# A prefetch hint on the closing branch of the four engines' loops over images

## The reference, cut to what matters

```python
x = _L0_conv_ref(x, ...)        # group norm, q/k/v, softmax(q k^T / sqrt(128)) v over 1024 points, projection, x + out
t = _to_tokens(x)               # 1024 tokens of 128 numbers
t = t + _L1_attn_ref(_ln_t(t), ...)   # 8 search heads x 2 retrievers of width 16, softmax over 1024 keys, gate, w_out
t = t + _L1_ffn_ref(_ln_t(t), ...)    # two 128x128 maps, one dequantised from 4 bits
x = _from_tokens(t, x)
```

## Time and profile before

| | |
|---|---|
| median of 3 executions | 5834.74 us (5830.56 to 5835.21) |
| the profiled execution | 5838.83 us, span 5836.5 us |
| busy: TensorE | 5436.7 us (93%), 30350 matmuls |
| busy: GpSimd | 4251.2 us (73%), 1109 instructions |
| busy: VectorE | 3955.0 us (68%), 8189 instructions |
| busy: ScalarE | 3470.2 us (59%), 6689 instructions |
| mean granted TensorE clock | 0.981 |

### The profile page before, as it was taken

The page is one execution under the profiler, slowest core; times in us unless marked ns, Lnnn a source line. Parts: engine busy times, 40 slices in busy tenths (PEclk is TensorE's granted clock), DMA queues, the critical chain, the costliest instruction groups (busy, mean ns, idle before and its releaser), DMA issues.

```text
span 5836.5 us, 99943 instructions
## 1 busy us (share of the span) xinstructions
PE 5436.7 (93%) x30350; PEld 3295.9 (56%) x30350; DVE 3955.0 (68%) x8189; ACT 3470.2 (59%) x6689; POOL 4251.2 (73%) x1109
## 2 busy tenths in 40 slices
PE   5999999999999999999999999999999999999986
PEld 3555555565555555555555555555555555556543
DVE  4776667667676666676667676677766676766763
ACT  2566566656566565666565665666665656665654
POOL 1677777777777777777777777777777777777787
PEclk9999999999999999999999999999999999999998
DMA  1101110111111111111111111111111111101110
GB/s 36 24 26 33 31 38 26 27 34 27 38 26 34 27 34 30 37 26 30 31 27 38 31 29 27 34 30 38 26 34 27 27 37 36 28 24 36 23 33 11
DMA packets 64867, 176.65 MB, mean 30 GB/s; under 512 B 21856, under 2 KB 23264, under 8 KB 64224
## 3 DMA queue, kind: packets, MB, share of 16 engines
q1 hardware_dynamic: 64224, 168.61, 12.3%
HBM read 17.53 MB, written 16.78 MB: 6 GB/s over the span
## 4 chain that ended last, share of the span: by engine, by line
PE 79%; DVE 9%; ACT 5%; issue 4%; POOL 2%; SPq 0%; DMA 0%; DVEq 0%; ACTq 0%; POOLq 0%
PE ps_bank L776 16%; PE ps_u L810 16%; PE ps_bank L799 15%; PE ps_bank L763 7%; PE ps_bank L691 4%; PE ps_bank L679 3%; DVE max_part L1062 3%; DVE max_part L1072 3%; PE ps_bank L747 2%; PE ps_bank L819 2%; PE ps_bank L750 2%; PE ps_bank L749 2%; PE ps_bank L748 2%; POOL p_sum L627 2%; ACT work L963 2%
## 5 line engine op out<-in xcount | busy, mean ns | idle before, releaser
L627 POOL TENSOR_TENSOR p_sum<-p_sum,p 128x2048 f32<-128x2048 f32 x768 | 3509.0, 4569 | 411.4 <-ACT p L982 381.2
L1072 DVE TENSOR_REDUCE max_part<-ps_bank 128x1 f32<-128x512 f32 x4096 | 2613.7, 683 | 1237.9 <-PE ps_bank L776 1224.9
L982 ACT ACTIVATE p<-ps_bank 128x512 f32<-128x512 f32 x4096 | 2283.6, 599 | 1495.3 <-PE ps_bank L799 1482.6
L799 PE MATMUL ps_bank<-q_stack,k_stack 128*128 128x512 f32 x4096 | 1726.3, 438 | 25.1 <-DVE t_front L1096 20.7
L776 PE MATMUL ps_bank<-k_stack,q_stack 96*128 96x512 f32 x4096 | 1594.6, 426 | 25.9 <-DVE max_part L1072 11.2
L776 PEld LDWEIGHTS ps_bank<-k_stack,q_stack 96*128 96x128 f32 x4096 | 777.6, 193 | 687.5 <-DVE max_part L1072 287.2
L627 POOL TENSOR_TENSOR p_sum<-p 128x2048 f32<-128x2048 f32 x128 | 584.3, 4565 | 792.4 <-ACT den_sb L990 731.3
L799 PEld LDWEIGHTS ps_bank<-q_stack,k_stack 128*128 128x128 f32 x4096 | 766.2, 192 | 655.1 <-issue 273.2
L810 PE MATMUL ps_u<-p,rv 128*32 128x512 f32 x8192 | 1114.5, 617 | 19.1 <-ACT u_sb L987 12.2
L763 PEld LDWEIGHTS ps_bank<-v,p 128*128 128x128 f32 x4096 | 494.1, 191 | 17.8 <-issue 2.4
L763 PE MATMUL ps_bank<-v,p 128*128 128x129 f32 x4096 | 498.2, 274 | 1.6 <-ACT p L939 1.6
(11 more groups left out here) (140 smaller groups left out, 4600.2 us busy)
## 6 DMA issues: line engine op xcount, KB each, us to landing
q_stack<-q_hi SPq DMA_DIRECT2D x256, 128.0 KB, 2.4
k_stack<-k_hi SPq DMA_DIRECT2D x512, 64.0 KB, 2.3
x_sb<-in_x SPq DMA_DIRECT2D x32, 512.0 KB, 3.3
t_held<-t_front SPq DMA_DIRECT2D x32, 512.0 KB, 2.9
k_stack<-k_lo SPq DMA_DIRECT2D x256, 64.0 KB, 2.4
q_stack<-q_lo SPq DMA_DIRECT2D x128, 128.0 KB, 2.3
t_core<-t_held SPq DMA_DIRECT2D x32, 512.0 KB, 3.4
out_y<-out_sb SPq DMA_DIRECT2D x32, 512.0 KB, 2.6
```

Source lines behind the costliest of these rows:

```text
L627: pool.tensor_tensor(p_sum[:, :, :], before, p1[:, step % ring, :, :], ALU.add)\
L799: pe.matmul(out, k_stack[:, head, keys], q_stack[:, head // 2, queries], start=True, stop=True)\
L982: act.activation(p1[:, step % ring, n, :], read_bank(), ACT.Exp, scale=scale1)\
L1072: dve.tensor_reduce(max_part1[:, i, n, half:half + 1], read_bank(), AXIS.X, ALU.max)\
```

## The change

`in_order` gets `nc` as its first argument, opens the loop through it with the same bounds and the one engine, and asks for a hint.

```diff
-def in_order(engine, steps, images, stages, banks=None, links=None, first=None):
+def in_order(nc, engine, steps, images, stages, banks=None, links=None, first=None):
...
     before = links.count if links else 0
-    with engine.Fori(1, images - 2) as b:
+    with nc.Fori(1, images - 2, engines=[engine.engine], hint_back_edge=True) as b:
         if banks:
             banks.looped = (b - 1) * (banks_per_image // BANKS)
...
-                in_order(pool, steps, images, {"values": add_weights, "norm_group_var": rstd0,
+                in_order(nc, pool, steps, images, {"values": add_weights, "norm_group_var": rstd0,
                                                "ln1_stats": rstd_shift(0), "ln2_stats": rstd_shift(1)})
...
-                in_order(pe, steps, images, stages, banks, first=first_of_image)
+                in_order(nc, pe, steps, images, stages, banks, first=first_of_image)
...
-                in_order(act, steps, images, stages, banks)
+                in_order(nc, act, steps, images, stages, banks)
...
-                in_order(dve, steps, images, stages, banks, links)
+                in_order(nc, dve, steps, images, stages, banks, links)
```

## The result

The changed kernel takes 5740.45 us in the median of 4 runs (5738.39 to 5743.39); the kernel before took 5833.13 us beside it. The ratio is 0.9842, with a 95% interval of 0.9825 to 0.9859: 93 us or 1.6% faster. The forecast was 5728 us, in a range of 5690 to 5765. The profiled execution took 5743.39 us, 95.4 us less than the one of before, where the sum said 107.

What follows compares the result with a forecast made beforehand. TensorE was taken to bound the kernel, idling at each loop branch and then running at a lower clock. 5838.8 - 85 (idle) - 22 (clock) = 5732 us for the profiled execution, 5728 us as a median; range 5690 to 5765.

Steps and rivals of the forecast that it cites:

- The bound and the gap: TensorE's 28 "issue" waits before L747, 87.7 us, come from its loop branch; the hint saves 85 us.
- The step behind it: Round's end on TensorE: branch, way to L747 and hint take 0.53 us, hidden behind 0.65 us of queued work.
- What is late next: Round's start: L810, L799 and L819 have 0.7, 0.6 and 4.9 us to spare, so no wait replaces the gap.
- ScalarE and VectorE: At the back edge: their hints cost nothing; unhinted, ScalarE would be 1.5 us late at L939, mostly soaked up by six banks.
- The clock: TensorE's lower clock goes behind the back edge but comes near L715 in 20 of 28 rounds: 22 us saved.
- The last round and the tail: Last branch falls through though hinted as taken: nothing in the sum, 4 us kept for the range.
- The hint without effect: Rival at the loop branch: hint forgotten or its fetch thrown out; 5837 us, chance 0.09.
- Code displaced ahead of the branch: Rival "slower": target's fetch displaces code of L747 to L784, costing 88 us; 5922 us, chance 0.04.
- The shrunken stall: Rival at the round's start: target or next block late, half of the 3.13 us stays; 5781 us, chance 0.07.

Runs made afterwards that it cites:

- e12: As e9, but the hint on TensorE's loop alone: 5666.66 us.
- e2: Changed kernel with the hint on VectorE, ScalarE and GpSimd, none on TensorE: 5834.83 us.
- e3: Changed kernel with L715's transposes placed 0.4 of a step later, which also put L672 first in step 19: 5779.42 us.
- e8: As e3, with max_rows0 (L736) at 0.75 instead of 0.95 of step 28: 5771.09 us.
- e9: As e3, but norm_group_var (L672) keeps its place as last of step 19 and only L715 moves: 5657.15 us.
- e11: As e9, with max_rows0 (L736) at 0.75 instead of 0.95 of step 28: 5652.62 us.
- e1: Changed kernel with the hint on TensorE's loop alone: 5736.75 us.
- e4: Kernel before, without any hint, with the same later place of L715 as e3: 5919.38 us.
- e10: Kernel before, without any hint, with L715 moved as in e9: 5791.3 us.
- e5: Changed kernel with all four hints at the start of step 31, not the top of the round, 5.3 us ahead of TensorE's branch: 5741.76 us.
- e6: Changed kernel with all four hints ahead of the round's last stage, 2.4 us ahead of TensorE's branch: 5832.12 us.
- e7: Changed kernel with all four hints ahead of the fourth stage of step 31, 3.9 to 4.1 us ahead of TensorE's branch: 5769.8 us.

## Why the prediction was right

The parts of the sum were 85 us of idle time and 22 us of clock, 107 in all. Measured were 87.0 and 15.4 us in the loop, and 7.3 us lost behind it, where the sum had nothing: 95 us.

**The bound and the gap.** Right. The 28 waits on "issue" were the branch's, and nearly all of their 87.7 us went; the 0.1 us a round that the forecast left over is not there. The step behind it was a little off and did not matter: from the branch to L747 it takes 0.61 us (2071.0 to 2071.61) where the sum was 0.53. TensorE's hinted branch is longer, at 0.36 us, than the 0.3 us taken from GpSimd's rows. The queued work, which ends at 2071.63, still covers it. The Trainium skill's compare-and-branch of 108 ns (Advanced Engine Details and Errata, Control Flow Timing) fits neither: in the two kernels the recorded ones take 45 to 63 ns in the median on three engines, and 357 on TensorE with the hint.

**What is late next.** Right: L810 and L799 follow without a wait, and GpSimd keeps its room.

**ScalarE and VectorE.** Right for the loop, where their hints cost nothing; behind the loop VectorE's and GpSimd's, costed at nothing, did not come free (see the last round). For the loop the forecast said that an unhinted ScalarE would be 1.5 us late at L939 and the banks would soak up most of it: it is 1.29 us late and 0.47 get through (e12).

**The clock.** The mechanism was right and the size too high: 15.4 us in the loop where 22 were forecast. The term that was mis-sized is the number of rounds that keep the lower clock near L715: I took 20 of 28, it was 24. At the forecast's own 1.76 us a round that gives 57 - 42 = 15 us. Per round the lower clock costs 1.50 us (174.30 - 172.80).

**The last round and the tail.** The part that I had taken at nothing in the sum, with 4 us in the range for one fetch at the branch: 7.3 us, almost twice that, and in another place. No branch pays: TensorE falls through in 88 ns, as before in 83. Instead VectorE stands still for 1.4 us and GpSimd for 2.6 us, well behind it. The two waits stand in the six kernels whose VectorE and GpSimd are hinted at the top of the round (the changed one, e2, e3, e8, e9, e11). They are missing in the five whose VectorE and GpSimd have no hint (before, e1, e4, e10, e12), and in e5, e6 and e7 too, whose late hints say taken of the same branch that falls through. So they come with a hint at the top of the round on these two engines; why, and what each costs without the other, is open.

**The rivals.** The hint without effect is out for a hint at the top of the round, and with it the reading of the Trainium skill (Runtime: NRT & Kernel Launch, Instruction fetch mechanics) by which prefetch is purely sequential: 3585 ns became 357. Code displaced ahead of the branch shows nowhere. The shrunken stall did not come about here; e7 made it, as a mixture of whole stalls and none, with two rounds between.

## What to carry to other kernels

Look at the closing branch of a long hardware loop on the engine that bounds the kernel: if its record is some microseconds long, or the next register instruction stands that far behind it, hint it, at the top of the body; on engines beside it the same stall is hidden until the first one is cured. An engine whose branch does not stall, as GpSimd's here, has nothing to win by a hint, and in all six kernels with one at the top of its round it stood still once for 2.6 us behind the loop. Count with a gap of TensorE also the slower clock behind it, and look for the next longest gap of the round (here 1.9 us), which may inherit it: here the two cures together gave 174 us, the hint alone 93 and the moved stage alone 40. When a stage is moved in a planned order, compare the whole step's order before and after, since the stages behind it move too.

## What the runs showed that I had not expected

- A hint 2.4 us ahead of TensorE's branch saves nothing of a 3.5 us stall; at 4 us of lead 19 rounds of 28 are cured, and at 5.3 us 26. In the changed kernel it stands a whole round, some 174 us, ahead, and all 28 are.
- A hinted branch on TensorE takes 357 ns, on the other engines 49 to 61.
- 10 us more of idle time in the one long gap of a round (2.3 us in place of 1.9, e3) went with 39 us more time. With both that gap and the back edge's stall in the round (e4) the kernel is 84 us slower than before, though its moved stage was meant to save 54.
- With hints at the top of the round, VectorE and GpSimd each stand still once behind the loop, 1.4 and 2.6 us.
